# Half-row score matmuls and two-bank maxima in an attention kernel on one core

## The reference, cut to what matters

```
xn  = group_norm(x1) * gamma + beta                      # per batch element, 512 x 1024
q, k, v = split(W_qkv @ xn + b)                          # 8 heads of 64 channels, 1024 positions
w   = softmax((q * s)^T (k * s))                         # per head 1024 x 1024, s = 64 ** -0.25
out = x1 + W_proj @ (w applied to v) + b_proj
```

## Time and profile before

| | us |
|---|---|
| median of 3 runs | 2893.01 |
| lowest, highest | 2890.81, 2893.12 |
| profiled execution, whole | 2894.75 |
| its span, first to last instruction | 2893.2 |
| PE busy | 2768.7 (96%) |
| VectorE busy | 1854.5 (64%) |
| ScalarE busy | 1243.0 (43%) |
| GpSimd busy | 1142.5 (39%) |

### The profile page before, as it was taken

One profiled execution on the slowest core, in us unless ns is written; L12 is line 12 of the kernel. 1 busy time (PEld: TensorE's weight loads), 2 busy tenths in 40 slices (PEclk: granted clock), 3 DMA queues, 4 the chain that ended last, 5 costly groups with the idle time before them and its releaser, 6 DMA issues.

```text
span 2893.2 us, 36061 instructions
## 1 busy us (share of the span) xinstructions
PE 2768.7 (96%) x11860; PEld 1816.3 (63%) x11860; DVE 1854.5 (64%) x2429; ACT 1243.0 (43%) x1535; POOL 1142.5 (39%) x531
## 2 busy tenths in 40 slices
PE   8999999998999999999999989999999899999998
PEld 6888878886655655575457545655665465557555
DVE  5554445555677557847774777478657856774776
ACT  3232222223456245525553464356345525553443
POOL 3310000001455355616661654355345625661662
PEclk9999999998999999999999999999999999999999
DMA  5331011121001110121012011201110121012001
GB/s 182 127 107 58 29 43 43 58 91 69 15 23 52 60 44 26 48 89 37 19 36 100 23 37 44 74 22 37 52 67 22 51 76 44 18 40 102 15 15 59
DMA packets 59315, 155.94 MB, mean 54 GB/s; under 512 B 8704, under 2 KB 8704, under 8 KB 59136
## 3 DMA queue, kind: packets, MB, share of 16 engines
q1 hardware_dynamic: 55552, 141.07, 13.9%
q0 software_dynamic: 3584, 12.58, 1.3%
HBM read 111.69 MB, written 41.94 MB: 53 GB/s over the span
## 4 chain that ended last, share of the span: by engine, by line
PE 81%; DVE 10%; issue 5%; ACT 3%; POOL 0%; ACTq 0%; DVEq 0%; POOLq 0%
PE psum L1103 16%; PE psum L1324 13%; PE psum L1285 13%; PE psum L1309 11%; PE psum L1291 8%; DVE small L938 6%; PE psum L1122 6%; PE psum L1146 3%; PE psum L1174 3%; PE psum L1338 2%; PE psum L1217 2%; PE psum L1114 1%; ACT a_all L671 1%; PE psum L1220 1%; PE psum L1358 1%
## 5 line engine op out<-in xcount | busy, mean ns | idle before, releaser
L506 POOL TENSOR_TENSOR a_all<-a_all 128x1024 f32<-128x1024 f32 x441 | 1066.6, 2418 | 1098.5 <-ACT a_all L671 786.3
L938 DVE TENSOR_REDUCE small<-psum 128x1 f32<-128x512 f32 x1024 | 687.3, 688 | 280.0 <-PE psum L1291 275.0
L671 ACT ACTIVATE a_all<-psum 128x1024 f32<-128x1024 f32 x512 | 512.4, 1024 | 439.0 <-PE psum L1309 425.3
L1309 PE MATMUL psum<-r_all 128*128 128x512 f32 x2048 | 599.4, 398 | 21.0 <-ACT a_all L671 18.4
L1291 PE MATMUL psum<-r_all 128*128 128x512 f32 x1024 | 440.3, 436 | 60.3 <-DVE small L938 46.0
L1324 PE MATMUL psum<-a_all 128*64 128x512 f32 x2048 | 496.8, 606 | 0.0
L1103 PE MATMUL psum<-r_all 128*128 128x512 f32 x1920 | 463.4, 402 | 4.9 <-DVE r_all L1004 4.9
L1309 PEld LDWEIGHTS psum<-r_all 128*128 128x128 f32 x2048 | 383.8, 189 | 118.7 <-ACT a_all L671 33.4
L1103 PEld LDWEIGHTS psum<-r_all 128*128 128x128 f32 x1920 | 368.7, 194 | 100.2 <-DVE a_all L963 11.4
L1291 PEld LDWEIGHTS psum<-r_all 128*128 128x128 f32 x1024 | 190.0, 188 | 329.7 <-DVE small L938 166.0
L1285 PE MATMUL psum<-r_all 128*128 128x512 f32 x1536 | 386.7, 401 | 10.7 <-DVE r_all L1023 5.5
(11 more groups left out here) (117 smaller groups left out, 2030.3 us busy)
## 6 DMA issues: line engine op xcount, KB each, us to landing
r_all<-w_dram SPq DMA_DIRECT2D x48, 1024.0 KB, 5.1
a_all<-y_dram SPq DMA_DIRECT2D x9, 2048.0 KB, 7.9
a_all<-x SPq DMA_DIRECT2D x16, 1024.0 KB, 6.3
y_dram<-a_all SPq DMA_DIRECT2D x16, 1024.0 KB, 4.2
out<-a_all SPq DMA_DIRECT2D x32, 512.0 KB, 3.0
a_all<-y_dram SPq DMA_DIRECT2D x56, 256.0 KB, 2.7
w_dram<-r_all POOLq DMA_DIRECT2D x16, 512.0 KB, 3.0
a_all<-w POOLq DMA_DIRECT2D x16, 256.0 KB, 3.0
```

The costliest lines, as they stand in the source:

```text
L506: pool.tensor_tensor(p_sum[:, h], probs[:, 0, h] if i == 1 else p_sum[:, h], probs[:, i % 2, h], ALU.add).then_inc(sum_step, 1)
L671: act.activation(probs[:, i % 2, h], psum[h][:, :, :].rearrange("p a n -> p (a n)"), ACT.Exp, scale=SCALE).then_inc(probs_ready, 1)
L938: dve.reduce_max(max2[:, h, tile, half:half + 1], ps, AX_X).then_inc(work_free, 1)
L1309: last = pe.matmul(psum[h][:, half], k, q[:, half * HALF:(half + 1) * HALF], start=first, stop=not first)
```

## The change

- Scores by half rows: for each half of 512 queries, four products (HI.HI, LO.HI, HI.LO, and ones times minus the maxima `mx`), each as one matmul for each head that uses only the head's own 64 contraction rows. The two heads' matmuls follow one another, use different rows of the array and write different banks. psum0 and psum1 now hold a half of the queries for both heads, and not a head. So a key tile is 16 matmuls with 64 rows in place of 8 with 128.
- A maximum product is two matmuls with 64 rows, one for each head, into both banks of psum3; VectorE reduces both banks in one instruction (128 x 2 from 128 x 2 x 512). There are 16 of these in a pair instead of 32 single ones, one behind each score half. `next_pair` counts two tiles, and `max_tile` waits for `work_free` of n - 2, which is the reduction of the maximum before it.
- Key tiles go two at a time: four score halves each followed by a maximum product, then two `weigh` calls (of the tile before the last and of the one before that; one in the first round, three after the last). `probs` has three slots.
- `max_turn`, the previous pair's `sums` (now into psum2, behind `o_ready`) and the four q and k tiles all stand ahead of the pair's scores. `max_rows` writes `mx` in one instruction.
- ScalarE writes the high part of a q or k tile in one instruction of 128 x 512; the copies of k and q are gone, and of ten memsets of padding rows on GpSimd one is left. VectorE writes the low part in one instruction. Both inversions of the sums stand ahead of the maxima, and `normalise`, `hid_lo` and `norm_lo` among them.
- Exponentials and GpSimd adds take 128 x (2 heads x 512 queries): the same count and size as before.
- In layer 0 the buffer `xt` shares memory with `gs` and `us`, with one more wait on `g_full`.

The core of the diff, in which the TensorE part comes last:

```diff
@@ buffers @@
+        xt = gs.rearrange("p a j c -> p (a j) c").rearrange("p (s a) c -> p s a c", a=2)
...
-        k_b = r1.take(2, 2, N)
-        q_b = r1.take(2, N)
+        q_hl, k_hl = r1.take(2, 2, N), r1.take(2, 2, N)
+        mx = r1.take(N)
+        ones_r = r1.take(P)
...
+        probs = a1.take(SLOTS, 2, N)
...
@@ gpsimd: the adds @@
+                            pool.wait_ge(probs_ready, ONE + pairs * 2 * NT + 2 * i + half + 1)
+                            pool.wait_ge(sum_step, ONE + pairs * ADDS + (i - 1 if last_pair else 2 * (i - 1) + half))
+                            pool.tensor_tensor(p_sum[:, :, cols], probs[:, 0, :, cols] if i == 1 else p_sum[:, :, cols],
+                                               probs[:, i % SLOTS, :, cols], ALU.add).then_inc(sum_step, 1)
...
@@ scalar @@
-            def qk_hi(b, pair, par, i, count):
+            def qk_hi(pair, par, i):
...
-                bias = bqkv_c[:, of_k * CT + pair:of_k * CT + pair + 1]
-                to = (q_a, k_a)[of_k]
-                for h in range(2):
-                    rows_ = slice(h * D, h * D + D)
-                    act.activation(to[rows_, par, h, cols], ps[rows_, :], ACT.Identity, bias=bias[rows_]).then_inc(qk_hi_done, 1)
-                if of_k:
-
-                    for h in range(2):
-                        act.wait_ge(qk_hi_done, 2 * (count + i) + h + 1)
-                        rows_, others = slice(h * D, h * D + D), slice(D - h * D, 2 * D - h * D)
-                        act.activation(k_a[others, par, h, cols], f(k_a[rows_, par, h, cols]), ACT.Copy).then_inc(k_twice, 1)
...
+                act.activation((q_hl, k_hl)[of_k][:, par, HI, cols], ps, ACT.Identity,
+                               bias=bqkv_c[:, of_k * CT + pair:of_k * CT + pair + 1]).then_inc(qk_hi_done, 1)
...
+                        for half in range(NH):
+                            cols = slice(half * HALF, (half + 1) * HALF)
+                            act.wait_ge(scores_full, pairs * 2 * NT + 2 * i + half + 1)
...
+                            else:
+                                if half == 0:
+
+                                    act.wait_ge(pv_done, ONE + pairs * NT + before + 1)
+                                if more:
+                                    act.wait_ge(sum_step, ONE + pairs * ADDS + 2 * (max(before, 1) - 1) + half + 1)
...
+                            act.activation(probs[:, i % SLOTS, :, cols], psum[half][:, :, :], ACT.Exp,
                                            scale=SCALE).then_inc(probs_ready, 1)
...
+                            hid_hi(b, p - 1, i - 2)
                         if p == 2 and not last:
...
@@ vector @@
-                for h in range(2):
-                    rows_, others = slice(h * D, h * D + D), slice(D - h * D, 2 * D - h * D)
-                    to = k_b[rows_, par, h, cols] if of_k else q_a[others, par, h, cols]
-                    dve.wait_ge(qk_hi_done, 2 * (count + i) + h + 1)
-                    ins = dve.scalar_tensor_tensor(out=to, in0=ps[rows_, :], scalar=bias[rows_],
-                                                   in1=f((q_a, k_a)[of_k][rows_, par, h, cols]),
-                                                   op0=ALU.add, op1=ALU.subtract)
-                ins.then_inc(work_free, 1)
-
-            def max_tile(t):
-
-                n, ps = work.next()
-                h, tile, half = t // (NT * NH), t // NH % NT, t % NH
+                to = (q_hl, k_hl)[of_k]
+                dve.wait_ge(qk_hi_done, count + i + 1)
+                dve.scalar_tensor_tensor(out=to[:, par, LO, cols], in0=ps,
+                                         scalar=bqkv_c[:, of_k * CT + pair:of_k * CT + pair + 1],
+                                         in1=f(to[:, par, HI, cols]), op0=ALU.add, op1=ALU.subtract).then_inc(work_free, 1)
+
+            def max_tile(m):
+
+                n = work.next_pair()
+                half, tile = m // NT, m % NT
                 dve.wait_ge(work_full, n)
-                dve.reduce_max(max2[:, h, tile, half:half + 1], ps, AX_X).then_inc(work_free, 1)
+                dve.reduce_max(max2[:, :, tile, half], psum[3][:, :, :], AX_X).then_inc(work_free, 2)
 
             def max_join():
 
                 dve.wait_ge(work_free, work.upto())
-                dve.reduce_max(max_cols[:, 0:2, 0:NT], max2, AX_X).then_inc(max_ready, 1)
...
-                    of = ps[32 * h:32 * h + NT, 0:P].unsqueeze(1).to_broadcast([NT, NT, P])
-                    to = q_b[D - h * D:D - h * D + NT, h].rearrange("p (j t) -> p j t", j=NT)
-                    ins = dve.tensor_tensor(to, of, mask[32 * h:32 * h + NT, :, :], ALU.mult)
-                ins.then_inc(work_free, 1)
+                dve.tensor_tensor(mx.rearrange("p (j t) -> p j t", j=NT), ps[:, 0:P].unsqueeze(1).to_broadcast([P, NT, P]),
+                                  mask[:, :, :], ALU.mult).then_inc(work_free, 1)
 
             def v_tile(b, i):
...
                     next_qk(0)
+                    max_rows(pairs)
                     if p:
+                        invert_sums(pairs - 1, 0)
                     next_qk(1)
                     if p:
+                        invert_sums(pairs - 1, 1)
                     next_qk(2)
                     next_qk(3)
+
+                    def between(m):
+                        if p:
+                            if m in (0, 1):
+                                normalise(pairs - 1, m)
+                            if m in (6, 8):
+                                hid_lo(b, p - 1, (m - 6) // 2)
+                        if p == 1 and m == 4 and not last:
+
+                            dve.wait_ge(xn_hi_done, (b + 1) * NH * CT)
+                            for i, of in enumerate((xn_scale, xn_bias)):
+                                dve.tensor_copy(next_norm[:, i], of[:, :, bass.ds(b + 1, 1)].rearrange("p j a -> p (j a)")).then_inc(next_norm_ready, 1)
+                        if p == 2 and not last:
+                            for u in range(NH * CT):
+                                if LO_AT[u] == m:
+                                    norm_lo(b + 1, u)
...
@@ tensor @@
-            def max_tile(par, t):
-                h, tile, half = t // (NT * NH), t // NH % NT, t % NH
-                pe.matmul(next_tile(), q_a[:, par, h, tile * P:(tile + 1) * P],
-                          k_a[:, par, h, half * HALF:(half + 1) * HALF], start=True, stop=True).then_inc(work_full, 1)
+            def max_tile(par, m):
+                half, tile = m // NT, m % NT
+                n = work.next_pair()
+                pe.wait_ge(work_free, n - 2)
+                for h in range(2):
+                    rows_ = slice(h * D, (h + 1) * D)
+                    last = pe.matmul(psum[3][:, h], q_hl[rows_, par, HI, tile * P:(tile + 1) * P],
+                                     k_hl[rows_, par, HI, half * HALF:(half + 1) * HALF], start=True, stop=True)
+                last.then_inc(work_full, 2)
 
...
-
-            def weigh(b, p, i, between):
+                keys = slice(i * P, (i + 1) * P)
+                for half in range(NH):
+                    cols = slice(half * HALF, (half + 1) * HALF)
+
+                    pe.wait_ge(probs_ready, ONE + pairs * 2 * NT + (2 * (i - 1) + half + 1 if i else 0))
+                    for t, (k, q) in enumerate(((k_hl[:, par, HI, keys], q_hl[:, par, HI, cols]),
+                                                (k_hl[:, par, LO, keys], q_hl[:, par, HI, cols]),
+                                                (k_hl[:, par, HI, keys], q_hl[:, par, LO, cols]),
+                                                (ones_r, mx[:, cols]))):
+                        for h in range(2):
+                            rows_ = slice(h * D, (h + 1) * D)
+                            last = pe.matmul(psum[half][:, h], k[rows_], q[rows_], start=(t == 0), stop=(t == 3))
+                    last.then_inc(scores_full, 1)
...
+                                         probs[:, i % SLOTS, h, half * HALF:(half + 1) * HALF], start=(i == 0), stop=(i == NT - 1))
+                last.then_inc(pv_done, 1)
+
+            def sums(pairs, last=False):
+
+                pe.wait_ge(o_ready, ONE + pairs + 1)
...
+                    pe.wait_ge(sum_step, ONE + (pairs + 1) * ADDS)
+                for half in range(NH):
+                    for h in range(2):
+                        last = pe.matmul(psum[2][h * D:(h + 1) * D, half], ones64, p_sum[:, h, half * HALF:(half + 1) * HALF],
+                                         start=True, stop=True)
+                last.then_inc(sums_full, 1)
...
+                    next_qk(0)
+                    turned = max_turn(pairs)
+                    if p:
+                        sums(pairs - 1)
+                    for i in range(1, QK):
+                        next_qk(i)
+
+                    pe.wait_ge(work_free, turned)
...
+                        scores(pairs, par, i, next_max)
+                        if i % 2:
+                            if i > 1:
```

(9 more changed lines are left out.)

332 lines of the change are left out of this document (117 added, 215 removed).

## The result

The changed kernel takes 3031.55 us (median of 4 runs, 3024.94 to 3040.46) against 2892.33 of the kernel before (four runs): 1.0484 of it, interval 1.0451 to 1.0517. My forecast was 2942, slower by 49, with a range up to 3020; the time lies above the range. The profiled execution took 3040.46 with a span of 3038.9, 145.7 more than before. Times in this document are medians of all executions; three executions (10143 us with half reductions, 9479 with filling, 2910.86 in the last run) were in a slower state, and without them those medians are 2765.79, 3002.89 and 2885.55.

What follows compares the result with a forecast made beforehand. Scoring was to be bound by 1.80 us maximum round trips, TensorE standing 0.66 us in each. +45.5 for seven batch elements, +4.7 for the last and -1.5 for the first pair gave +48.7: 2942 us, range 2868 to 3020.

Steps and rivals of the forecast that it cites:

- A: Rival: the row halves run one after the other, TensorE bounds the scoring, 51.8 us against 43.9: 3190 us; chance 8%.
- B: Rival: the row halves overlap in part, at a slot of 0.30 us: 3014 us; chance 8%.
- C: Rival: the two-bank reduction costs less than the slope says; at 1.05 us, 2879 us in all; chance 12%.
- D: Rival: VectorE's helpers meet idle GpSimd and drains are smaller, 1.5 us less a pair: 2895, no change; chance 6%.
- So a round trip takes 1.80 us: From one maximum product through its two-bank reduction to the next: 0.50 + 0.03 + 1.22 + 0.05 us.
- 5.6 for `norm_lo`: Pair p = 2: eight `norm_lo` at a mean of 1.30 us join and add 5.6, six of them in short gaps.
- the first pair of all: 16 round trips (28.8 us) against 31 steps of four slots (28.2), less some 2 for copies of k: -1.5.
- the fourth pair of the last batch element: Took 37.2 us before with TensorE waiting for the inversions; forecast to change by -4.
- the helpers' price: VectorE operations between reductions: `normalise` twice 0.1 us, one `hid_lo` behind two `weigh`, the other 0.9, `norm_lo` 5.6 in p = 2.
- Rides in the 0.58 that the next maximum takes to come: `normalise`, 0.69 us alone on VectorE, fits in the wait for the next maximum and costs twice 0.1 us.
- The account of pairs: Sum of scoring and the work ahead of it for a batch element's four pairs: +3.5, +1.6, -0.2, +1.6 us.
- `hid_lo` and `norm_lo` at both bounds 2 us a pair: Part of the grounds for the sum's own range, 2905 to 2990, beside 37 us for 0.1 of round trip.

Runs made afterwards that it cites:

- half reductions: Changed kernel, each reduction of the maxima reading only the first 256 columns of each of the two banks: 2766.34 us.
- filling: Changed kernel plus two more pairs of half-row matmuls, their result overwritten, before each score half in a gap without `weigh`: 3003.71 us.
- the last run: Changed kernel with a wait, bank and reduction for each head's maximum, scale copies and `hid_lo` moved, and added half-row products before score halves: 2890.07 us.
- a ring of two: Changed kernel, each head's maximum with its own wait, count and one-bank reduction, so one bank fills while the other is reduced: 2904.98 us.
- short adds: GpSimd's adds cut from the third key tile on: changed kernel (64 of each head's 512 columns) 2906.13 us; kernel before (128 of 1024) 2848.68.

## Why the prediction was wrong, step by step

- **The mechanism was right.** The reduction of two banks takes 1.224 (forecast 1.22), the half rows run side by side at the full slot, TensorE waits for a reduction 12 times a pair, neither TensorE nor ScalarE waits for GpSimd, and the time went up for that reason: half a reduction takes 265 us off, a ring of two 126, and 57 of the 139 us stay when the adds are short. Rivals A, B, C and D are out: A and B by the 1.10 us for eight half-row matmuls, C by the 1.224, D because helpers met a busy GpSimd more often, not less.
- **"So a round trip takes 1.80 us".** It takes 1.89: 0.52 + 0.09 + 1.24 + 0.04. I had let VectorE start 0.03 behind the product; it starts 0.09 behind (1631.38 plus 0.52, then 1631.99). At 12 gaps in 31 pairs the 0.09 too little are 33 us. It was offset elsewhere in the sum, because with short adds the two kernels differ by 57 us where I had 49, and by 6.9 instead of 6.5 in a batch element. That is luck in part: the sum has 5.6 for `norm_lo` in it, and with short adds the pair with `norm_lo` takes 1.4 longer than the one before it. Two small terms were missed as well: the first pair of all, which I had at -1.5, takes 41.2 against 37.1, and the fourth pair of the last batch element, at -4, takes 37.4 against 37.2.
- **The step that failed is the helpers' price, with the clock that hangs on it.** I wrote that the second `hid_lo` "costs 0.2 to 1.8, I take 0.9", took `norm_lo` at the mean of the kernel before, "1.30", and did not count the copies of the next scale at all, as they took 0.16. Measured, a round with the second `hid_lo` or with the copies is 2.3 or 2.1 longer, and `norm_lo` means 1.84. Even the bound of 1.8 was too low: the longest `hid_lo` is 2.85 here. A mean length was carried over from a schedule in which fewer of these operations met an add. The earlier trace rows had the maxima of 2.55 and 2.41 in view, and lengths like these were the price here: at the places shown the add began 0.1 us ahead of the helper, which then stood behind nearly all of it. Short adds take 125 us off the changed kernel and 42 off the one before, so of the 139 us these collisions, with what they do to the clock, are 83. That is nearly all of what I missed.
- **TensorE's clock was taken as unchanged, without a word.** It fell from 0.986 to 0.961, behind rounds of 9 us with 6 to 7 us of work. At least 28 us hang on it, by the filled gaps, and `weigh` alone is 45 us longer than at 0.988. In the last pair shown it counts for more than the collision: the round is 2.3 us longer, and the two `weigh` behind it 2.7 (6.30 against 3.58), which together are about the 4.9 between this pair's 61.5 and the 56.6 with short adds. It is not a cause of its own: with short adds it is 0.988 without any other edit.
- **Cover in the sum.** "Rides in the 0.58 that the next maximum takes to come" held for short helpers only. The account of pairs was 55.6, 57.1, 62.7, 57.1; with short adds they are 56.2, 56.6, 58.0, 56.6 (means of seven), with whole ones 56.2, 63.1, 66.0, 60.4. The one pair without helpers, p = 0, was off by 0.6.
- **The range** had "`hid_lo` and `norm_lo` at both bounds 2 us a pair". The sum fell short by more: by 6.0, 3.3 and 3.3 us for p = 1 to 3 in the mean, since the copies and the clock were in neither bound, and the second `hid_lo` sits in a gap without `weigh`.

## What to carry to other kernels

Where a change turns a buffered exchange between two engines into a strict round trip, a small operation that sits between is paid as far as it outlasts the other engine's work (here `normalise` at 0.69 was free, `hid_lo` at 2.8 cost 2.3); price each by its longest row as well as its mean, and look for what makes the longest one long. If two engines share a way into memory, put the colliding operation where the waiting engine has other work (here the rounds' two `weigh`), and keep a ring of two even if one joint instruction is cheaper. Price what the clock loses behind such a wait, too: in the last pair shown it lost 2.7 us where the wait had lost 2.3. And run a control of the kernel before with the same edit: 125 us of gain mean little until one knows that the old kernel gains 42.

## What the runs showed of the hardware that I had not expected

- Two matmuls of 64 rows each, in different halves of the rows and to different banks, run fully side by side: eight of 512 columns in 1.10 us with the drain, the time of four.
- A VectorE copy of 128 x 4 elements, 0.16 us alone, took 2.30 when a GpSimd add had begun 0.11 us before it, about that add's length (mean of all 14: 1.23, since the second of each two follows the first at once).
- A round of 9.29 us in which TensorE was busy for 5.95, with 2.43 us as its longest pause, was followed by mostly 1.2 GHz (granted clock 0.57 over 1846.90 to 1853.20), and two `weigh` took 6.30 instead of 3.58; adding work that nobody needs made the kernel 28 us faster.
